# Setup of two attention stages gathered into one block each, matmul order in them, and taps in halves in the delta stage

## The reference

```python
x = x + _L0_attn_ref(_layernorm(x), ...)   # delta rule: 16 heads of 64, convolution of 4 taps, state per head
x = x + _L0_ffn_ref(_layernorm(x), ...)    # 8 experts, top 1, and a shared one
x = x + _L1_attn_ref(_layernorm(x), ...)   # window attention: 16 heads of 8, 64 keys back, initial keys and values
x = x + _L1_ffn_ref(x, ...)                # layer norm, full attention within 256 tokens, then 8 experts, top 2
```

```python
# window: q, k, v = x @ Wq.T, x @ Wk.T, x @ Wv.T; k and v get last_k_init, last_v_init ahead
scores = einsum('blhd,blwhd->blwh', q, k_win) * dh ** -0.5
out = einsum('blwh,blwhd->blhd', softmax(scores, axis=2), v_win).reshape(b, l, d) @ Wo.T
# full: h = layernorm(x, g, b); q, k, v = split(h @ w_qkv + b_qkv)
attn = softmax(einsum('bqhd,bkhd->bhqk', q, k) / sqrt(DK), axis=-1)
x = x + einsum('bhqk,bkhd->bqhd', attn, v).reshape(B, S, D) @ w_o + b_o
```

## Time and profile before

| What | Value |
|---|---|
| median of 3 runs | 6774.56 us (6771.26 to 6777.18) |
| the profiled execution's own time | 6762.3 us |
| its span, first to last instruction | 6760.5 us |
| TensorE, busy share of the span | 86% |
| vector engine, ScalarE, POOL | 55%, 49%, 37% |
| delta stage's main loop, about | 130 to 4100 us |
| first experts, about | 4100 to 4519 us |
| window stage | 4519 to 5311 us |
| full stage | 5311 to about 6150 us |

### The profile page before, as it was taken

One profiled execution on the slowest core, in us unless ns is written; L12 is line 12 of the kernel. 1 busy time (PEld: TensorE's weight loads), 2 busy tenths in 40 slices (PEclk: granted clock), 3 DMA queues, 4 the chain that ended last, 5 costly groups with the idle time before them and its releaser, 6 DMA issues. The chain is left out here.

```text
span 6760.5 us, 187448 instructions
## 1 busy us (share of the span) xinstructions
PE 5798.9 (86%) x67109; PEld 4366.6 (65%) x67110; DVE 3719.7 (55%) x7246; ACT 3294.8 (49%) x7154; POOL 2518.8 (37%) x2359
## 2 busy tenths in 40 slices
PE   5999999999999999999999996757888588885586
PEld 4676676666766766667667665555666466664486
DVE  5555555555555555555555555554444466665443
ACT  2555555555555555555555552232333255552165
POOL 5545444544454445454544453340000100003553
PEclk9999999999999999999999998889999799996598
DMA  3000000000000000000000001120000000001124
GB/s 95 21 22 18 18 22 22 18 18 22 21 18 18 21 22 18 18 21 22 18 18 22 22 18 33 30 72 1 0 0 0 2 0 0 0 0 38 37 62 122
DMA packets 99340, 161.01 MB, mean 24 GB/s; under 512 B 19973, under 2 KB 82245, under 8 KB 96069
## 3 DMA queue, kind: packets, MB, share of 16 engines
q1 hardware_dynamic: 76260, 121.44, 6.0%
q0 software_dynamic: 14080, 26.64, 1.2%
q10 hardware_dynamic: 8320, 4.19, 0.2%
HBM read 118.03 MB, written 104.87 MB: 33 GB/s over the span
## 5 line engine op out<-in xcount | busy, mean ns | idle before, releaser
L789 PE MATMUL bank<-wc,hT 128*128 128x512 f32 x2088 | 1043.4, 615 | 47.3 <-issue 28.7
L956 PE MATMUL bank<-X,kqe 128*128 128x64 f32 x6240 | 775.7, 278 | 75.0 <-DVE rb L1451 54.5
L956 PEld LDWEIGHTS bank<-X,kqe 128*128 128x128 f32 x6240 | 727.8, 192 | 99.1 <-DVE rb L1451 70.1
L1189 ACT ACTIVATE TT<-bank 128x512 bf16<-128x512 f32 x640 | 382.3, 597 | 664.0 <-PE bank L937 661.6
L1491 DVE TENSOR_TENSOR yb<-bank,masks 128x512 bf16<-128x512 f32 x768 | 526.3, 686 | 179.8 <-PE bank L919 172.5
L789 PEld LDWEIGHTS bank<-wc,hT 128*128 128x128 f32 x2088 | 352.4, 191 | 310.2 <-issue 282.0
L1289 POOL TENSOR_TENSOR qa<-qa,qt 128x512 f32<-128x512 f32 x390 | 486.9, 1269 | 34.8 <-POOL qt L1284 34.8
L1430 DVE TENSOR_TENSOR kqe<-bank,ex 128x512 f32<-128x512 f32 x520 | 335.1, 686 | 274.8 <-PE bank L863 274.8
L1189 ACT ACTIVATE T<-bank 128x512 bf16<-128x512 f32 x640 | 348.9, 595 | 272.1 <-PE bank L930 270.2
L1322 POOL TENSOR_SCALAR_AFFINE_SELECT kqe<-kqe 128x512 f32<-128x512 f32 x260 | 215.7, 830 | 642.5 <-DVE kqe L1430 642.5
L919 PEld LDWEIGHTS bank<-T,mTb 128*128 128x128 bf16 x6144 | 264.2, 99 | 263.9 <-ACT T L1189 106.0
(11 more groups left out here) (531 smaller groups left out, 13256.5 us busy)
## 6 DMA issues: line engine op xcount, KB each, us to landing
sent_l0f<-blank_l0f SPq DMA_DIRECT2D x64, 528.0 KB
sent_l1m<-blank_l1m SPq DMA_DIRECT2D x64, 528.0 KB
xin<-sent_l1m SPq DMA_DIRECT2D x139, 66.0 KB
taken_l1m<-back_l1m SPq DMA_DIRECT2D x16, 512.0 KB, 8.7
xin<-sent_l0f SPq DMA_DIRECT2D x75, 66.0 KB
decay_sums<-decay_rows SPq DMA_DIRECT2D x264, 3.0 KB
cw_stage<-in_L_attn_conv_w_dram SPq DMA_DIRECT2D x4, 1024.0 KB, 6.4
out_dram<-x_sb ACTq DMA_DIRECT2D x8, 512.0 KB, 7.0
```

What stands on the lines that cost most here:

```text
L789: mm = pe.matmul(bk[:, :], src[:, j:j + P], w["wc"][:, j, at * 512:(at + 1) * 512], start=(j == 0), stop=(j == TAPS - 1))
L956: mm = pe.matmul(bk[:, i * D0:(i + 1) * D0], lhsT(hh), rhs(hh), start=True, stop=True)
L1189: nc.scalar.activation(dst, bk[:, :].rearrange("p (h a u) -> p h a u", h=8, u=1 << l), ACT.Copy).then_inc(actb.done.sem, 1)
```

## The change

In `norm_stats` a caller may give every engine something to do beside the statistics, and `later` keeps all powers but those of the first four tiles out of it. The window and full stages have one block for weights, constants and statistics. In it SP issues the first part of taken_win, then the weights, then the other parts; POOL makes all memsets; ScalarE copies and pads (`pad_heads`), from PSUM where the weight was turned. The powers left over are taken on POOL in the main loop, four tiles in a body, ahead by a body. In the main loop `project_out` stands ahead of `weigh`, and in odd tiles `turn_h` ahead of `turn_back`. In the delta stage taps 2 and 3 of v1 and the gate z1 are computed in halves of 256 columns: one half between the joins of the two groups, the other where the whole stood (z1: behind `turn_h`).

```diff
@@ -165,11 +166,20 @@
                         lo = (ch * tiles + i * n) * P
                         sp.dma_start(got[:, ch, i * n:(i + 1) * n, :],
                                      back[lo:lo + n * P, :].rearrange("(t p) d -> p t d", p=P)).then_inc(arrived[i], 16)
-            if sync:
+                    if i == 0 and sync:
+                        sync(sp)
+            elif sync:
                 sync(sp)
...
@@ -216,12 +226,13 @@
             if pool_first:
                 pool_first(pool)
             k = 0
-            for i in range(2):
-                T = slice(i * half, (i + 1) * half)
+            for i in range(1 if later else 2):
+                T = slice(0, 2 * TPB) if later else slice(i * half, (i + 1) * half)
                 pool.wait_ge(var_ready, i + 1)
                 for j, m in ((1, twice), (0, mr)):
                     if m is not None:
-                        pool.tensor_tensor(m[:, 1, T], var[:, j, T], c["halves"][:, 0:half], ALU.pow).then_inc(powered, 1)
+                        pool.tensor_tensor(m[:, 1, T], var[:, j, T], c["halves"][:, 0:T.stop - T.start], ALU.pow
+                                           ).then_inc(powered, 1)
                         k += 1
             pool.wait_ge(powered, k)
...
@@ -781,14 +792,16 @@
                 bk = actb.fill(pe, b, name)
                 pe.transpose(bk[:, 0:P], h, c["ident"][:, :]).then_inc(actb.full.sem, 1)
-            def taps(b, src, ch, first, count):
+            def taps(b, src, ch, first, count, half=None):
+                cols = slice(0, 512) if half is None else slice(half * 256, half * 256 + 256)
                 at = {"k": 0, "v": 2}[ch[0]] + int(ch[1])
                 bk = proj.fill(pe, b, ch) if first == 0 else proj.banks[(proj.filled - 1) % 2]
                 for j in range(first, first + count):
-                    mm = pe.matmul(bk[:, :], src[:, j:j + P], w["wc"][:, j, at * 512:(at + 1) * 512],
-                                   start=(j == 0), stop=(j == TAPS - 1))
-                if first + count == TAPS:
+                    mm = pe.matmul(bk[:, cols], src[:, j:j + P], w["wc"][:, j, at * 512 + cols.start:at * 512 + cols.stop],
+                                   start=(j == 0), stop=(j == TAPS - 1 and half != 0))
+                if first + count == TAPS and half != 0:
                     mm.then_inc(proj.full.sem, 1)
             def query_chunks(b, src, i):
...
@@ -816,11 +829,14 @@
                 pe.matmul(bk[:, 0:H0], sums_q[:, :], c["ident"][0:H0, 0:H0], start=True, stop=True
                           ).then_inc(dveb.full.sem, 1)
-            def gate_tap(b, ch):
+            def gate_tap(b, ch, half=None):
                 at = int(ch[1])
-                bk = proj.fill(pe, b, ch)
-                pe.matmul(bk[:, :], hTz, w["wz"][:, at * 512:(at + 1) * 512], start=True, stop=True
-                          ).then_inc(proj.full.sem, 1)
+                cols = slice(0, 512) if half is None else slice(half * 256, half * 256 + 256)
+                bk = proj.banks[(proj.filled - 1) % 2] if half == 1 else proj.fill(pe, b, ch)
+                mm = pe.matmul(bk[:, cols], hTz, w["wz"][:, at * 512 + cols.start:at * 512 + cols.stop], start=True,
+                               stop=True)
+                if half != 0:
+                    mm.then_inc(proj.full.sem, 1)
             def turn_heads(b, src, name):
                 for half in range(2):
...
@@ -1024,13 +1040,17 @@
                     for l in range(1, LEVELS):
                         step = {1: "r1", 2: "r2", 3: "r3", 4: "r4", 5: "o"}.get(l)
                         for G in range(2):
+                            if l == 2 and G == 1:
+                                taps(b, hT[t % 2], "v1", 3, 1, 0)
                             join_a(b, t, l, G)
                             if l > 1:
                                 join_tt(b, t, l - 1, G)
+                            if l == 1 and G == 1:
+                                taps(b, hT[t % 2], "v1", 2, 1, 0)
                             if step:
                                 solve(b, t, step, G)
                             if l == 4:
-                                gate_tap(b, f"z{G}")
+                                gate_tap(b, f"z{G}", 0 if G == 1 else None)
                             if l == 6:
                                 if t % 2 == 1:
                                     state(b, t, G)
@@ -1043,9 +1063,10 @@
                             else:
                                 join_last(b, t, G)
                         if l <= 2:
-                            taps(b, hT[t % 2], "v1", l + 1, 1)
+                            taps(b, hT[t % 2], "v1", l + 1, 1, 1)
                         if l == 4:
                             turn_h(b, t + 2, "h")
+                            gate_tap(b, "z1", 1)
                         if l == 5:
                             query_squares(b, t + 1)
                     turn_squares(b, t)
...
+    def sync(sp):
+        for dst, src in first:
+            sp.dma_start(dst, src).then_inc(first_in, 16)
+        for dst, src in rest:
+            sp.dma_start(dst, src).then_inc(rest_in, 16)
+        sp.wait_ge(blank, 1)
+        sp.dma_start(to_blank, from_blank).then_inc(rest_in, 16)
+    def gpsimd(pool):
+        pool.memset(flat(w["last_v" if window else "ob"]), 0.0).then_inc(blank, 1)
+        for v in (wq, wk, qb, spread):
+            pool.memset(flat(v), 0.0).then_inc(zeroed, 1)
+        pool.memset(flat(va), 0.0).then_inc(pstep, 1)
+        for v in zeros:
+            pool.memset(flat(v), 0.0).then_inc(pstep, 1)
         for v in ones:
+            pool.memset(flat(v), 1.0).then_inc(pstep, 1)
+        n = 1 + len(zeros) + len(ones)
+        pool.wait_ge(pstep, n)
+        pool.memset(va[:, :, :, :, DH], 1.0).then_inc(pstep, 1)
+        n += 1
         if window:
...
+    def vector(dve):
+        dve.tensor_reduce(neg[:, :], c["ident"][:, TOP_ROW::GROUP], AX, ALU.add).then_inc(neg_ready, 1)
+        dve.wait_ge(neg_ready, 1)
+        dve.tensor_scalar(neg[:, :], neg[:, :], -1.0, None, ALU.mult).then_inc(neg_ready, 1)
+    def scalar(act):
+        act.wait_ge(zeroed, 4)
         if window:
+            act.wait_ge(rest_in, 16 * (len(rest) + 1))
+            pad_heads(nc, spread[0:LEAD, :, :], w["last_k"][0:LEAD, :], spread_ready, SETS)
+            nc.scalar.activation(by_slot[:, :, :, :], w["wo_cols"].rearrange("p (g s d) -> p s g d", g=GROUPS, s=SLOTS),
+                                 ACT.Copy).then_inc(cols_ready, 1)
+            act.wait_ge(turned, 1)
+            pad_heads(nc, wq[:, :, :], wbank[:, 0:P], astep, SLOTS)
+            pad_heads(nc, wk[:, :, :], wbank[:, P:2 * P], astep, SETS)
+            nc.scalar.activation(w["wv"], wbank[:, 2 * P:3 * P], ACT.Copy).then_inc(astep, 1)
+            act.wait_ge(turned, 2)
+            act.wait_ge(neg_ready, 2)
+            for p in range(2):
+                nc.scalar.activation(kT[:, p, :, 0:LEAD], bank[:, 0:SETS * LEAD].rearrange("p (s n) -> p s n", s=SETS),
+                                     ACT.Identity, bias=neg[:, :]).then_inc(astep, 1)
+            for i in range(SETS):
+                nc.scalar.activation(qb[:, SLOTS + i:SLOTS + i + 1], neg[:, :], ACT.Copy).then_inc(astep, 1)
+            act.wait_ge(turned, 3)
+            nc.scalar.activation(w["wo"], obank[:, 0:P], ACT.Copy).then_inc(astep, 1)
...
+    def tensor(pe):
         if window:
+            pe.wait_ge(first_in, 16 * len(first))
+            for i in range(3):
+                mm = pe.transpose(wbank[:, i * P:(i + 1) * P], w["rows"][:, i, :], c["ident"][:, :])
+            mm.then_inc(turned, 1)
+            pe.wait_ge(spread_ready, SLOTS)
+            for i in range(n_parts):
+                mm = pe.transpose(bank[:, i * LEAD:(i + 1) * LEAD], spread[0:LEAD, i, :], c["ident"][0:LEAD, 0:LEAD])
+            mm.then_inc(turned, 1)
...
+    return {"sync": sync, "pool_first": gpsimd, "vector_first": vector, "scalar": scalar, "tensor": tensor}
...
-                                zeros=(wq, wk, qb, va, mxp, hT, mr[:, :, tiles:], x_all[:, tiles + 1:, :],
-                                       x_all[:, 0, :], *(() if mid is None else (mean[:, :, 0], mid[:, 0, :]))),
-                                ones=(oT, ones))
+            beside = attention_constants(
+                nc, c, early, tag, w, window, loads, wq=wq, wk=wk, qb=qb, va=va, kT=kT, band=band, bandT=bandT,
+                zeros=(mxp, hT, mr[:, :, tiles:], x_all[:, tiles + 1:, :], x_all[:, 0, :],
+                       *(() if mid is None else (mean[:, :, 0], mid[:, 0, :]))),
+                ones=(oT, ones, var[:, :, tiles:]))
+            if mid is None:
+                norm_stats(nc, c, x_sb, mr, tiles, 1e-5, tag, take=take, later=var, **beside)
+            else:
+                norm_stats(nc, c, x_sb, mean[:, :, 1:], tiles, 1e-5, tag, twice=mr, later=var, **beside)
```

(24 more changed lines are left out.)

173 lines of the change are left out of this document (57 added, 116 removed).

## The result

| | before | after |
|---|---|---|
| median of four executions each, us | 6775.87 (6771.26 to 6779.31) | 6684.93 (6668.84 to 6700.43) |
| ratio, 95% interval | | 0.9868 (0.985 to 0.9885) |
| profiled execution, its span | 6762.3, 6760.5 | 6692.99, 6691.0 |
| mean granted clock | 0.949 | 0.939 |

What follows compares the result with a forecast made beforehand. TensorE was taken as the only engine near its limit, so time could come from its idle stretches, loop waits and clock. 24 + 35 + 48 + 37 + 48 = 192 us less gave 6583 us, range 6545 to 6640.

Steps and rivals of the forecast that it cites:

- 1 and 2, the changes of stage: Setups ahead of the window and full attentions: one block each starts h sooner, 24 us and 35 us less.
- The stall that I took at 1.0 us: Change into window: weight loads on SP delay later parts of taken_win, stalling the vector engine 1.0 us, bounds 0 and 2.6.
- rival C: Changes of stage keep half their length, as POOL and the vector engine hold each other up: 6613 us; chance 0.08.
- the 2 us that I had charged: Change into window: POOL held up 2.0 us for each of four vector-engine sums, inside the cover.
- 3, delta: Delta stage: half taps fill TensorE's waits and let joins come earlier, 0.75 us a tile, 48 us less; bounds 19 to 60.
- rival A: Delta's halves don't pay, as ScalarE's T or the vector engine's yb moves behind each join: 6631 us; chance 0.2.
- 4, window: Window loop: early project_out gains 0.99 us a tile, less turn_h's cost; 1.2 a pair, 37 us less, bounds 20 to 60.
- turn_h's cost: Window loop, every second tile: turn_back starts 0.68 us later with turn_h first; a further 0.12 is taken off each pair.
- 5, full: Full loop: early project_out saves its 0.75 us wait a tile, turn_h first costs nothing; 48 us less, bounds 34 and 50.
- B: Full attention: the clock rises from 0.97 as the change takes idle out, 23 us over the stage, to 6560; chance 0.2.
- this stage has no long idle, and still falls: Sign against B: the full attention's clock is 0.97 although TensorE has no long idle there.
- D: Slower: z1 finishes behind turn_h, delaying POOL's and ScalarE's copies and the work queued behind; 6807 us; chance 0.02.

Runs made afterwards that it cites:

- e8: The change with its delta part undone (v1 taps and z1 gate whole again); 0.9923 of before, window loop 753.3 us, full loop 786.3.
- e2: The change with only turn_h undone (turn_back first again, both stages), project_out still early; 0.9755 of before, window loop 672.6 us, full loop 798.7.
- e10: The kernel before plus four unread transposes ahead of turn_h in every second full-stage tile; 0.9964 of before, full loop 769.7 us.
- e9: e2 plus four unread transposes ahead of scores and four ahead of turn_h in every second full-stage tile, window code untouched; 0.9700 of before, full loop 757.0 us.
- e1: The change with both main-loop edits (turn_h first, project_out early) undone in both stages; 0.9846 of before, window loop 735.6 us, full loop 797.9.
- e3: The change with only project_out undone (behind turned_scores again, both stages), turn_h still first; 0.9957 of before, window loop 811.1 us, full loop 791.5.
- e4: The change with both main-loop edits undone in the window stage alone; 0.9873 of before, window loop 734.4 us, full loop 787.0.
- e5: The change plus nine unread transposes ahead of turn_h's wait in every second window tile; 0.9833 of before, window loop 716.3 us.
- e6: e2 with the full stage's scores split, groups 2 and 3 ahead of the wait for the exponentials; 0.9745 of before, full loop 794.5 us.
- e12: e2 with z1's gate in one piece of 512 columns again, v1's halves kept; 0.9773 of before (two executions).
- e11: The change plus the unread transposes of e5 in window and of e9 in full; 0.9769 of before, window loop 714.4 us, full loop 757.1.
- e7: e2 plus the full-stage transposes of e9, with turn_h's bank reserved early in window too; 0.9742 of before, window loop 701.5 us, full loop 755.7.

## Why the forecast was wrong

**1 and 2, the changes of stage: right.** 25.8 and 34.9 us for 24 and 35. The stall that I took at 1.0 us wasn't there: the second sum stands directly behind the first half's statistics.

```profile
4489.88 2.29 DVE L191 TENSOR_TENSOR x_sb<-x_sb,taken_win 128x2048 f32<-128x2048 f32 x1 [6.03 <-DMA taken_win<-back_l0f]
4492.21 3.19 DVE L194 BATCH_NORM_STATS2 stats_win<-x_sb 128x6 f32<-128x128 f32 x16
4495.31 2.28 DVE L191 TENSOR_TENSOR x_sb<-x_sb,taken_win 128x2048 f32<-128x2048 f32 x1
...
4502.02 2.96 POOL L234 TENSOR_TENSOR mr_win<-variance_win,halves 128x4 f32<-128x4 f32 x1 [6.61 <-DVE variance_win L217]
```

The rival C, POOL and the vector engine in each other's way, didn't come: the sums kept 2.29 us. POOL's power took 2.96 us here, beside the third sum, and 1.01 alone in the loop: held up by the 2 us that I had charged, well inside its cover.

**3, delta: right.** 0.73, 0.6 to 0.67 and 0.73 a tile for 0.75, 43 us for 48; rival A falls. In after's TensorE, the join of level 2 follows 0.63 behind the half tap, and from r1.1 to that join it is 2.93 us (3.24 in the earlier trace rows); from the second join of level 2 to the first of level 3 2.09 (2.52): 0.31 and 0.43, forecast 0.30 and 0.45.

```profile
1999.83 2.00 PE L972 MATMUL bank<-X,kqe 128*128 128x64 f32 x16
...
2002.13 0.68 PE L802 MATMUL bank<-wc,hT 128*128 128x256 f32 x2
2002.76 0.41 PE L935 MATMUL bank<-T,mTb 128*128 128x64 bf16 x8
...
2003.98 0.40 PE L935 MATMUL bank<-T,mTb 128*128 128x64 bf16 x8
...
2006.07 0.40 PE L935 MATMUL bank<-T,mTb 128*128 128x64 bf16 x8
```

**4, window: the pair right, the loop wrong.** The terms stand: 1.97 for 1.98, and turn_h's cost 0.65 for 0.80. What failed is the step that isn't there: "a pair: 2 x 0.99 - 0.68 - 0.12 = 1.2, times 32" takes for granted that all 32 pairs run at the clock of before. I had written that turn_h first makes turn_back start 0.68 us later. That is the same as saying that TensorE's gap of 0.94 us grows to 1.44, and I priced the delay and not the gap. What the runs show in its place: a clock of 0.91 over this loop, which cost some 60 us (e8 less e2 less the delay), so that the loop became 24.7 us longer where 37 less were forecast.

**5, full: two steps failed.** The gain was put at 0.75 a tile, from start to start, and the 0.53 that the row showed was kept as the lower bound. The lower one is right, and for one tile in two. An undisturbed pair went from 22.99 to 22.56 us. The gain is in the tile that ends with keys (12.08 to 11.56 from turn_tops to turn_tops); the other got 0.1 longer. In the one that ends with values another wait took the place (timeline of after's TensorE; compare):

```profile
5758.76 1.15 PE L2901 MATMUL bank_full<-q_full,kT_full 17*128 17x256 f32 x16
5759.84 0.71 PE L2845 MATMUL bank_full<-wqkv,hT_full 128*128 128x128 f32 x4
5761.14 1.15 PE L2872 MATMUL bank_full<-kT_full,q_full 17*128 17x256 f32 x16 [0.59 <-ACT pr_full L3041]
5762.21 0.44 PE L2824 MATMUL bank_full<-ident,h_full 128*128 128x128 f32 x2
```

scores shares two banks with the turned scores and has to wait until ScalarE has read them; the wait for project_out's result had hidden that. I didn't ask what is late next in this tile. With the clock held in both, project_out's place is worth 769.7 - 757.0 = 12.7 us in this loop (e10 less e9), not 48. The waits of after over 700 us of this loop (waiting line, what it waits for; total us, times, longest) say the same:

```profile
PE bank_full L2937 <- DVE on_full L3140: 27.2, 53, 0.5
PE bank_full L2872 <- ACT pr_full L3041: 17.7, 30, 0.6
PE bank_full L2901 <- DVE mxp_full L3123: 16.5, 30, 0.6
```

And the clock took the rest: over the stretches of this loop it was 0.96 or 0.97 with project_out late (before, e1, e3) and 0.93 to 0.95 with it early (after, e2, e4, e5, e6). That idle time lowers it here too is shown by e9 and e10. The tile behind values has three gaps in both kernels. Before they are 0.53, 0.56 and 0.54 us, and the instructions behind them start 3.15 and 1.68 us apart; in after they are 0.59, 0.55 and 0.54, at 2.50 and 1.68. Whether this closer row is what lowers the clock further, with less idle time in all, was not tried by itself: e6 took out the first gap and left the other two, and the clock did not rise.

**The rivals.** B had the mechanism, a clock that follows idle time, and the wrong sign. It reckoned with the sum of the idle time, which the change does lower, and not with where the rest of it stands. The Trainium skill, TensorE: Matmul & The Clock Gate, Part 1, says that the throttled state is the default and activity releases it; e5, e9 and e10 agree (0.91, 0.93 and 0.97 became 1.00). What I had set against B, "this stage has no long idle, and still falls", was the very thing to take note of: short gaps are enough. D, by z1, did not come (e12). With the clock held, the change gives 0.9769 (e11), 6619 us on the scale of before, 36 short of 6583. In its trace 17 of them are in the window loop (714.4, where 734.4 - 37 = 697 was forecast), with the stalls at the jump back; 14 in the full loop (757.1 for 743). The delta stage gave 5 less than forecast. That the full loop lacks only 14 is luck of a sort: 22 of its 34 us are a clock that before did not have either (e10), and the forecast had none of it.

## What to carry to other kernels

Where the granted clock of a loop is below 1.00 or TensorE's gaps in it are near each other, an edit isn't priced by the undisturbed period alone: write down where its idle stands afterwards, and look at the granted clock of the loop as well as at its waits. A few matmuls whose result nobody reads, put in front of the wait that can't be avoided, are a test of this in one run, and a remedy: e9 (project_out early, turn_back first, eight fillers in every second tile of the full stage) takes 0.9700 of before, where e2, the same without the fillers, takes 0.9755 and the change 0.9868. And of two instructions that are ready at different times, the one that is ready first goes first; when a wait goes, ask for each kind of tile what is late next.

## What was not expected of the hardware

- TensorE's clock went to its lower level after a gap of 1.44 us that followed 5.7 us of unbroken work, and stayed there for 10 us of nearly unbroken work. The window loop ran at 0.91 with TensorE busy 88% of the time (573.35 of 650), and at 0.99 with 85% (527.07 of 620): the busy share alone does not tell the clock, the less so as a lower clock makes the same work busy for longer.
- Filling such gaps with useless work made loops shorter by 43 us (e5), 42 (e9 against e2) and 22 (e10 against before).
- Half of the groups of a packed matmul take as long as all four (e6: 1.13 us for 8 matmuls, 1.15 for 16).
- TensorE stands for 2.8 us at the jump back of some loops and not of others with the same work (e7 against e9), or even with the same code of the loop (the change against e8). Open.
